# A two-layer graph attention kernel: the second attention with features on partitions, probabilities divided ahead of their turns, turned rows in banks by token tile

## What is computed

```python
h = relu(layernorm(x))                       # x: [128, 64, 384]
# layer 0: 12 heads of 32, additive attention
v = einsum('bnd,ade->bane', h, W)
t = tanh(v)
a = leaky(t @ w_src + swap(t @ w_dst));  a = where(adj, a, -999)
f = elu(heads_to_features(softmax(a) @ v + b))
g = sigmoid(h @ H_w.T + H_b)
x = x + g * f + (1 - g) * h
h = relu(layernorm(x))
# layer 1: 6 heads of 64, dot-product attention
q, k, v = heads(h @ Wq + bq), heads(h @ Wk + bk), heads(h @ Wv + bv)
p = softmax(q @ k.T / 8 + where(adj, 0, -9e15))
x = x + features(p @ v) @ Wf + bf
```

## Time and profile before

| | |
|---|---|
| median of 3 runs | 1072.71 us (1072.68 to 1074.22) |
| profiled execution | 1072.87 us, its span 1070.8 us |
| TensorE matmul busy | 991.1 us, 93% of the span |
| TensorE weight load busy | 857.0 us, 80% |
| VectorE busy | 780.3 us, 73% |
| ScalarE busy | 574.5 us, 54% |
| GpSimd busy | 277.7 us, 26% |
| mean granted TensorE clock | 0.979 |

### The profile page before, as it was taken

How to read it: one execution, slowest core, us unless ns; L and a number is a source line. 1 busy time by engine, 2 the same in 40 slices (tenths; PEclk the granted TensorE clock), 3 DMA queues, 4 the chain that set the end, 5 groups by cost and what they waited for, 6 DMA issues and landing times.

```text
span 1070.8 us, 24885 instructions
## 1 busy us (share of the span) xinstructions
PE 991.1 (93%) x10153; PEld 857.0 (80%) x10153; DVE 780.3 (73%) x1456; ACT 574.5 (54%) x1126; POOL 277.7 (26%) x338
## 2 busy tenths in 40 slices
PE   6589999999999999999999999999999999999686
PEld 5487878888787887978788797878879788887575
DVE  4867867778786777868677886767788676876814
ACT  6556466373746636374564638446463754745331
POOL 2233140502415051240504124050321406032120
PEclk9689999999999999999999999999999999999988
DMA  9211151510414142031413204151241515111102
GB/s 237 32 15 20 29 90 32 90 32 31 61 32 91 31 82 40 31 62 32 91 32 77 41 12 83 31 91 31 65 39 19 91 32 90 32 47 18 28 30 59
DMA packets 183652, 56.41 MB, mean 53 GB/s; under 512 B 164978, under 2 KB 183540, under 8 KB 183540
## 3 DMA queue, kind: packets, MB, share of 16 engines
q1 hardware_dynamic: 183540, 54.83, 28.3%
HBM read 17.06 MB, written 12.58 MB: 28 GB/s over the span
## 4 chain that ended last, share of the span: by engine, by line
PE 55%; DVE 27%; ACT 7%; issue 7%; POOL 0%; ACTq 0%; DVEq 0%; POOLq 0%
PE ps L624 11%; PE ps L610 10%; PE ps L626 10%; PE ps L625 10%; DVE x L948 5%; PE ps L693 5%; PE ps L790 4%; DVE ee L945 4%; ACT p L430 3%; DVE hT1l L1056 3%; DVE hT0l L858 3%; DVE stats L842 3%; DVE p L973 2%; PE ps L808 2%; DVE x_in L996 2%
## 5 line engine op out<-in xcount | busy, mean ns | idle before, releaser
L410 POOL TENSOR_TENSOR x_in<-x_in,ee 128x384 f32<-128x384 f32 x64 | 72.5, 1134 | 626.7 <-DVE ee L951 626.7
L469 ACT ACTIVATE th<-ps 128x384 f32<-128x384 f32 x64 | 31.9, 499 | 209.8 <-DVE v_tok L936 209.8
L1020 DVE TENSOR_TENSOR hT1l<-ps,hT1h 128x512 fp32r<-128x512 f32 x48 | 30.4, 685 | 88.2 <-ACT hT1h L540 88.1
L984 DVE COPY_PREDICATED_SCALAR z<-not_adj,masked 128x768 f32 x64 | 69.4, 1084 | 32.5 <-ACT z L501 32.5
L610 PE MATMUL ps<-ident,p 128*128 128x128 f32 x576 | 76.3, 283 | 17.8 <-ACT p L430 10.0
L403 POOL TENSOR_TENSOR x_in<-x_in,h 128x384 f32<-128x384 f32 x64 | 85.5, 1367 | 18.5 <-DVE Wf_lo L883 18.5
L610 PEld LDWEIGHTS ps<-ident,p 128*128 128x128 f32 x576 | 65.3, 144 | 23.0 <-issue 12.7
L624 PE MATMUL ps<-Wf_hi,hT1h 128*128 128x384 f32 x192 | 69.0, 359 | 10.4 <-DVE hT1l L1056 10.4
L397 POOL TENSOR_TENSOR x_in<-x_in,bf_row 128x384 f32<-128x384 f32 x64 | 62.1, 1003 | 48.0 <-ACT p L430 48.0
L507 ACT ACTIVATE z<-z 128x768 f32<-128x768 f32 x64 | 54.5, 853 | 28.1 <-DVE z L989 28.0
L501 ACT ACTIVATE z<-ps 128x384 f32<-128x384 f32 x128 | 52.5, 497 | 31.0 <-PE ps L693 31.0
(11 more groups left out here) (130 smaller groups left out, 2796.5 us busy)
## 6 DMA issues: line engine op xcount, KB each, us to landing
V<-v_tok SPq DMA_DIRECT2D x128, 192.0 KB, 5.0
x_in<-in_x_dram SPq DMA_DIRECT2D x16, 768.0 KB, 5.0
out_dram<-x_in SPq DMA_DIRECT2D x16, 768.0 KB, 3.6
x<-in_L_gnn_H_w_dram SPq DMA_DIRECT2D x1, 576.0 KB, 5.9
QT<-in_L_gnn_W_dram SPq DMA_DIRECT2D x3, 192.0 KB, 6.7
thT<-in_L_gnn_Wq_dram SPq DMA_DIRECT2D x1, 576.0 KB, 5.8
z<-in_L_gnn_Wk_dram SPq DMA_DIRECT2D x1, 576.0 KB, 6.8
z<-in_L_gnn_Wv_dram SPq DMA_DIRECT2D x1, 576.0 KB, 7.9
```

The lines of the kernel that those rows point to most:

```text
L410: pool.tensor_tensor(x_in[:, i % 3, t], x_in[:, i % 3, t], ee[:, t], ALU.subtract).then_inc(x2_made, 1)
L984: dve.copy_predicated(zt, not_adj[:, t].unsqueeze(1).broadcast_to((P, HEADS0, N)), masked0[:].unsqueeze(2).broadcast_to((P, HEADS0, N))).t ...
```

## The change

The second attention is computed with features on partitions: V1 becomes the weight and the turned probabilities are streamed, so each result is already what the output product needs, and is not turned. The sums can't ride along in that form. So `divide1` works on the probabilities, ahead of their turns: a row sum, a reciprocal and a multiply over a pair of token tiles, twice per iteration. V1 loses its column of ones and is laid out by token tile b of a pair and row half, spread by eight DMAs instead of four. p1 gets gaps of 64 columns, so that one access covers the heads of a pair of tiles.

`attend1` writes bank b for token tile 2*pair + b. Head 2k + o goes to partitions 64*o on, and is read from row half o ^ b.

All turned rows (h0, tanh(h), h1) now sit in banks by token tile instead of by feature chunk: four jobs of 384 columns instead of three of 512. ScalarE copies and VectorE subtracts a token tile at a time (`high_tile`, `low_tile`), and the h0 and output products wait for their own tile. `project` first does all matmuls on high parts, then those on the low parts. The ring and the orders on TensorE, ScalarE and VectorE are rewritten to match; the last two h0 turns move behind the second attention, the first two ahead of the probability turns.

```diff
         RING = (
             [x for pair in pairs_of_jobs for x in pair]
-            + jobs("thT_copied", 0, thT_copied, 3)
-            + jobs("h1_low", 1, h1_low, 3)
+            + jobs("thT_copied", 0, thT_copied, 4)
+            + jobs("h1_low", 1, h1_low, 4)
...
             + jobs("probs0T_copied", 0, probs0T_copied, 6)
-            + jobs("attn0_made", 0, attn0_made, 4)[0:2]
+            + jobs("attn0_made", 0, attn0_made, 4)[0:3]
+            + jobs("h0_low", NEXT, h0_low, 4)[0:2]
             + jobs("probs1T_copied", 1, probs1T_copied, 3)
-            + jobs("attn0_made", 0, attn0_made, 4)[2:3]
-            + jobs("attn1_made", 1, attn1_made, 4)
             + jobs("attn0_made", 0, attn0_made, 4)[3:4]
-            + jobs("h0_low", NEXT, h0_low, 3)
-            + jobs("attn1_low", 1, attn1_low, 3)
+            + jobs("attn1_low", 1, attn1_low, 4)
+            + jobs("h0_low", NEXT, h0_low, 4)[2:4]
             + jobs("out_made", 1, out_made, 4)
         )
...
                     for g in range(2):
-                        for o in range(2):
-                            sp.dma_start(V1[64 * o:64 * o + 64, g].rearrange("p t k e -> p (t k) e")[:, :, 0:E1],
-                                         v_tok[64 * g:64 * g + 64].rearrange("p t (k o e) -> p (t k) o e", o=2, e=E1)[:, :, o])\
-                                .then_inc(values1_spread, 16)
+                        for r in range(2):
+                            for b in range(2):
+                                sp.dma_start(V1[64 * r:64 * r + 64, g, b].rearrange("p q k e -> p (q k) e"),
+                                             v_tok[64 * g:64 * g + 64, 2 * b:2 * b + 2]
+                                             .rearrange("p q (k o e) -> p (q k) o e", o=2, e=E1)[:, :, r ^ b])\
+                                    .then_inc(values1_spread, 16)
...
-            def h0_parts(g):
-
+            def high_tile(to, name, t):
+                toks = slice(t * P, (t + 1) * P)
+                return act.activation(to[:, :, toks], ps[:, job(name, t) % BANKS, 0:D].rearrange("p (c m) -> p c m", m=P), ACT.Copy)
+
+            def h0_parts(g, tiles):
...
+                if real(i + 1):
+                    h0_parts(i + 1, range(0, 2))
                 if real(j):
                     for c in range(3):
                         act.wait_ge(probs1_turned, 3 * j + c + 1)
                         act.activation(KT[:, c], ps[:, job("probs1T_copied", c) % BANKS], ACT.Copy).then_inc(probs1T_copied, 1)
                 exp_elu(0)
                 exp_elu(1)
+                exp_elu(2)
                 if real(j):
                     act.wait_ge(values1_full, TILES * (j + 1))
-                    for c in range(C):
-                        act.wait_ge(attn1_turned, C * j + c + 1)
-                        act.activation(hT1h[:, c], ps[:, job("attn1_low", c) % BANKS], ACT.Copy).then_inc(attn1_high, 1)
+                    for t in range(TILES):
+                        act.wait_ge(attn1_full, 2 * j + t // 2 + 1)
+                        high_tile(hT1h, "attn1_low", t).then_inc(attn1_high, 1)
...
-                    product(ps[:, job(name, o) % BANKS], lambda c: wh[w][:, c, cols], lambda c: wl[w][:, c, cols],
-                            lambda c: hT1h[:, c], lambda c: hT1l[:, c],
-                            chunk_ready=lambda c: (h1_low, C * j + c + 1)).then_inc(full, 1)
+                    dst = ps[:, job(name, o) % BANKS]
+                    pe.wait_ge(h1_high, TILES * (j + 1))
+                    for c in range(C):
+                        pe.matmul(dst, wh[w][:, c, cols], hT1h[:, c], start=(c == 0), stop=False)
+                        pe.matmul(dst, wl[w][:, c, cols], hT1h[:, c], start=False, stop=False)
+                    pe.wait_ge(h1_low, TILES * (j + 1))
+                    for c in range(C):
+                        mm = pe.matmul(dst, wh[w][:, c, cols], hT1l[:, c], start=False, stop=(c == C - 1))
+                    mm.then_inc(full, 1)
...
                 def attend1(pair):
 
-                    pe.wait_ge(values1_spread, 64 * (j + 1))
+                    pe.wait_ge(values1_spread, 128 * (j + 1))
                     pe.wait_ge(probs1T_copied, 3 * j + pair + 2)
-                    for o in range(2):
-                        take(i, job("attn1_made", 2 * pair + o))
-                    for t in range(2):
-                        for k in range(PAIRS1):
-                            q, at = divmod((2 * pair + t) * PAIRS1 + k, 4)
+                    for b in range(2):
+                        take(i, job("attn1_low", 2 * pair + b))
+                    for k in range(PAIRS1):
+                        for b in range(2):
+                            t = 2 * pair + b
+                            q, at = divmod(t * PAIRS1 + k, 4)
                             for o in range(2):
-                                rows = slice(64 * o, 64 * o + 64)
-                                bank = ps[:, job("attn1_made", 2 * pair + o) % BANKS, 0:HEADS1 * (E1 + 1)]\
-                                    .rearrange("p (t k e) -> p t k e", t=2, e=E1 + 1)
+                                rows = slice(64 * (o ^ b), 64 * (o ^ b) + 64)
                                 for g in range(2):
-                                    mm = pe.matmul(bank[g * N:(g + 1) * N, t, k], KT[rows, q, at * P + g * N:at * P + (g + 1) * N],
-                                                   V1[rows, g, t + 2 * pair, k], start=True, stop=True, skip_group_check=True)
+                                    mm = pe.matmul(ps[64 * o:64 * o + 64, job("attn1_low", t) % BANKS, k * P + g * N:k * P + (g + 1) * N],
+                                                   V1[rows, g, b, pair, k], KT[rows, q, at * P + g * N:at * P + (g + 1) * N],
+                                                   start=True, stop=True, skip_group_check=True)
                     mm.then_inc(attn1_full, 1)
...
-                def divide1(q):
+                def divide1(pair):
                     if real(j):
-                        pair, o = divmod(q, 2)
...
+                        probs = p1_pair(pair).rearrange("p t (h m) -> p t h m", m=N)
+                        sums = rs1[:, 2 * pair:2 * pair + 2]
+                        dve.wait_ge(probs1_made, TILES * j + 2 * pair + 2)
+                        dve.tensor_reduce(sums, probs, AX_X, ALU.add).then_inc(sums1_made, 1)
+                        dve.wait_ge(sums1_made, 2 * j + pair + 1)
+                        dve.reciprocal(sums, sums).then_inc(inv1_made, 1)
+                        dve.wait_ge(inv1_made, 2 * j + pair + 1)
+                        dve.tensor_tensor(probs, probs, sums.unsqueeze(3).broadcast_to((P, 2, HEADS1, N)), ALU.mult)\
+                            .then_inc(probs1_divided, 1)
```

More of the change, by code:

```diff
@@ L767, in body, with turn_probs @@
                     scores(1)
-                def turn_probs(name, ready, done, src, pairs, n, jobs):
+                def turn_probs(name, ready, made, done, src, pairs, n, jobs):
                     for q in range(jobs):
@@ L853, in norm0, with low_tile, h0_lows @@
                 row_sums(0, g)
[L855 to L859 removed]
+            def low_tile(to, high, name, t):
+                toks = slice(t * P, (t + 1) * P)
+                return dve.tensor_tensor(to[:, :, toks], ps[:, job(name, t) % BANKS, 0:D].rearrange("p (c m) -> p c m", m=P),
+                                         high[:, :, toks].bitcast(F32), ALU.subtract)
+            def h0_lows(g, tiles):
+                for t in tiles:
+                    dve.wait_ge(h0_high, TILES * g + t + 1)
+                    low_tile(hT0l, hT0h, "h0_low", t).then_inc(h0_low, 1)
             norm0(0)
@@ L1017, in body @@
                 if real(j):
-                    for c in range(C):
-                        dve.wait_ge(h1_high, C * j + c + 1)
-                        dve.tensor_tensor(hT1l[:, c], ps[:, job("h1_low", c) % BANKS], hT1h[:, c].bitcast(F32),
-                                          ALU.subtract).then_inc(h1_low, 1)
+                    for t in range(TILES):
+                        dve.wait_ge(h1_high, TILES * j + t + 1)
+                        low_tile(hT1l, hT1h, "h1_low", t).then_inc(h1_low, 1)
                 if real(i):
```

144 lines of the change are left out of this document (69 added, 75 removed).

## The result

The changed kernel takes **1059.1 us** (median of 4 runs, 1058.01 to 1060.95), against 1073.06 us (1072.68 to 1074.22) for the kernel before on the same chip: a ratio of 0.987, with an interval of 0.9853 to 0.9887. It is faster by 14 us, and the forecast was 1056.7 us in a range of 1048 to 1078. The execution that was profiled is the slowest of the four, 1060.95 us with a span of 1059.1 us, so that profile shows 11.7 us of the gain (1070.8 - 1059.1).

A forecast was written before the change was run, and what follows sets the result against it. VectorE, then ScalarE, bound the stretch from second attention to query product, TensorE the rest. 15 x 0.9 + 2.5 = 16 us off 1072.87 gives 1056.9; the runs' median is 0.16 lower: 1056.7 us, range 1048 to 1078.

The forecast's parts named there:

- What sets the period: Second attention to first query product: VectorE, then ScalarE, set the end while TensorE has slack; net 0.95 us per iteration.
- One of the prediction's signs of being wrong: TensorE's wait for th (tanh(h)) gone, which would mean that TensorE is the bound.
- attend1 starts 3.3 us later: Second attention on TensorE: waits for banks freed behind VectorE's added divides, starting at 558.9 instead of 555.56.
- VectorE's idle piece, and ELU 1.3 us earlier: VectorE idles 0.6 us ahead of the hT1l lows; first ELU step starts at 564.05 against 565.35.
- 4.15 us of divides: VectorE, between the mask and divide0(0): two divides of whole probability pairs, 2.1 us each, 4.15 us for two.
- 0.3 to 0.35 us given back: thT and hT1h copies: four of 384 instead of three of 512 elements; query product needs all four high tiles.
- The term that decides: attend1's new order costs nothing if work waits per quarter; rivals: pairs block (chance 0.24), one quarter at a time (0.06).
- V1's DMAs: Spread of V1 on SP: eight issues cost 3.7 to 7.4 us, taken as hidden; rival, V1 late, chance 0.06.
- The ends of the program: Start and last iteration together: 2.5 us of gain, bounds 5 and -1 us.
- I keep 0.6 us: Program start: h0 product needs only the first low part, two pitches of 0.6 us earlier; 0.6 us counted as gain.
- gains some 0.5 us in the same way: Start of the program: the first group's second h0 product gains some 0.5 us.
- I take 1.4 us for both: Last iteration: 2.32 us wait and 2.57 us turns go, 4.15 us divides come; last normalisation goes tile by tile; 1.4 us.

The follow-up runs named there:

- more_turns: Changed kernel with twelve more turns of the identity, into a bank that is overwritten, just ahead of the output product; 1064.56 us, ratio 0.9917.
- g_outer: Changed kernel with attend1's loop over g outside those over b and o, so four matmuls in a row go to four quarters; 1059.82 us, ratio 0.987.
- runs_of_six: Changed kernel with attend1's loops as b, o, k, g, so six matmuls in a row share a quarter; 1103.42 us, ratio 1.0283.

## Why the prediction was right

**What sets the period.** Right. VectorE and then ScalarE set it between 560 and 587, and TensorE's slack there hides its work: three runs of different make (turns removed, turns added, a divide moved) agree. One of the prediction's signs of being wrong did come, though: the wait for tanh is nearly gone, 3.8 us in 4 for 19.4 in 30. The sign was ill chosen. Counted from the scores, the chain came 1.15 us forward and TensorE's h0 products only 0.28 (21.54 to 21.26; 0.5 was forecast), so ScalarE no longer makes TensorE wait at its turns, and the slack shows at the query product, 0.75 us each time. Of the 1.47 us of more_turns this wait took 0.42, 0.5 went in ahead of tanh's turns and 0.3 among them (they took 1.77 us in the changed kernel and 1.47 there), and 0.20 showed in the period. How much of the 1.0 us comes from each part of the change (the turns gone, the banks by token tile, the new order) no run separates.

**attend1 starts 3.3 us later.** Measured 3.5. The banks set it, as forecast: the wait is on x of L941, divide0(2), 0.54 us. The turns of the second half of the probabilities wait 0.55 us for the second divide, where 1 us was forecast. What was missed is the 0.49 us ahead of attend0(2), which the profile puts down to issue. The code has it wait there for ScalarE's fifth copy of the turned z (L604, whose row starts at 486.37), 0.1 us behind whose end it starts; it too lies in the slack.

**VectorE's idle piece, and ELU 1.3 us earlier.** The piece is 0.87 us, not 0.6, and ELU comes 1.15 us earlier. Of the missing part, attend1 starts 0.13 us later than forecast, and its first pair takes 0.1 us more (0.81 for 0.71). The price of the 4.15 us of divides was right to 0.1: from 485.61 to 489.84 are 4.23 us.

**0.3 to 0.35 us given back.** In size too small, 0.4 us (from -1.40 at the thT copies to -1.00 at the query product), but -1.40 is more than ELU's -1.15. tanh's turns now go tile by tile, so that ScalarE's copies of thT follow its last gate without a gap: from the first normalisation to the first thT copy it was 4.14 us, now 3.88. I had not seen this 0.26 us. That the errors cancel is luck: net 1.00 in place of 0.95 us, which had been rounded to 0.9.

**The term that decides.** Right side taken, at a chance of 0.55 to 0.30. The rule of the Trainium skill (TensorE: Matmul & The Clock Gate, Part 3, The mechanism) that matmuls start and end strictly in program order isn't what these traces show of the starts, for float32 matmuls of 64 rows and 64 columns: with neighbours in one quarter, its order would leave two quarters working, 1.42 us a pair by the pace above, and 0.81 was measured, with four starts within 0.05 us. The other rule of the Trainium skill (TensorEngine Tiling (Array Packing), Gotcha 1), that row tiles can't use one PSUM bank at a time, doesn't hold in this form either: in g_outer the two row halves alternate within a bank, at different partitions, and a pair takes the 0.71 us that it took before, when each row half had a bank of its own.

**V1's DMAs.** Right: 6.69 us of issue for eight lie in the forecast's 3.7 to 7.4, a piece lands a median of 2.4 us after its issue, where one of twice the size took 4.5, and attend1 never waits for V.

**The ends of the program: wrong in sign.** The step that failed is "I keep 0.6 us" and "gains some 0.5 us in the same way", and "I take 1.4 us for both" for the last iteration. The start lost 2.34 us in the profiled run. The sum took matmuls that start earlier as matmuls that end earlier, at one pace. In the second iteration TensorE was early only for a longer wait, with half the clock behind it (1 us, shown); at the very start the slower pitch lasted longer, in some runs. At the end 0.3 us came out (1.0 less 0.7), not 1.4. TensorE's first probability turns of the last iteration, before and after:

```profile
1048.48 0.87 PE L610 MATMUL ps<-ident,p 128*128 128x128 f32 x6 [2.27 <-ACT p L512]
```

```profile
1041.43 1.51 PE L629 MATMUL ps<-ident,p 128*128 128x128 f32 x6 [5.95 <-DVE p L953]
```

The sum had the divides "partly beside the exponentials"; they are nearly all in the way. attend1 starts 11.07 us after the last scores instead of 7.40, 3.7 of the 4.15 us of divides, and the wait and turns that go are 4.9 us (2.32 + 2.57). The interval before it came out 0.7 us longer, for a reason that no run shows, and with a last interval that varies from 55.1 to 58.0 us over the profiles of the changed schedule (runs_of_six aside) the sign of the whole end isn't sure. All in all the ends gave -2 instead of +2.5 us in the profiled execution, 4.5 us apart, a little more than the 4.1 us by which it missed its own forecast (1060.95 against 1056.9). The median of the runs missed by 2.4 us.

**The count of periods.** The sum took 15 x 0.9 = 13.5 us; there are 14 full periods of 0.98, 13.7 us. Two small errors, one against the other.

## What to carry to other kernels

On a chain that passes from engine to engine, a removed instruction is worth what it brings forward at the next handover; a run that removes it without doing its work elsewhere measures just that. Read the busiest engine's waits before trusting its busy share: at 92 to 93%, TensorE hid 1.27 of 1.47 us of added turns, and moving a single divide into VectorE's idle piece gave 8 us more. A wait that goes away on one engine isn't proof that this engine is now the bound; see first whether it has moved to the next handover. Work that only becomes ready earlier can make one wait out of two short ones, and the matmuls behind a long wait may be at half the clock.

## What the runs showed of the hardware that was not expected

- Float32 matmuls of 64 x 64 on different quarters of the array overlap although neighbours in the order share a quarter, but with a limited reach: 48 records start within 0.71 us with alternating quarters, 0.81 in pairs, 2.16 in runs of six.
- A wait of 2.63 us, with 0.52 us of turns and then 0.23 us of waiting behind it, was followed by a granted clock of 0.52 (the 1.2 GHz level) from 80.8 to 84 us. The same stretch after a wait filled with 20 turns had 1.00. In the changed kernel's steady iterations the longest wait of TensorE is 0.75 us, and the granted clock is 1.00 from 120 to 900 us. At the start of g_outer a wait of 2.52 us was followed by 1.00 for 1.4 us and then by 0.50 from 20.6 to 23.8.
- At the start of the program the pitch of the matmuls told of the 1.2 GHz level (0.32 us for 384 columns) where the granted clock read 1.00, from 14 to 19 us before and up to 22.3 us in the changed kernel. From 20.6 to 23.8 us in g_outer the two agree (0.32 us and 0.50).
- Halving a DMA does not halve its issue: 3.70 us for four, 6.69 us for eight, 0.93 and 0.84 us each; but the landing came down from 4.5 to 2.4 us.
